# Sixteen expert blocks moved into the last batch's routing, and experts taken in the order of their rows

## The reference, cut to what matters

```
x = x + attention(layernorm(x))            # 16 heads of 16, causal, rotary
t = layernorm(x)
scores = softmax(t @ Wg.T)                 # 16 experts in 4 groups
topi   = top_k(scores, where the two best groups are, 4)
y = sum over the token's 4 experts of scores[e] * (silu(t@W1[e]) * (t@W3[e])) @ W2[e]
z = (silu(t@Ws1) * (t@Ws3)) @ Ws2          # shared expert, every token
x = x + y + z
```

## Time and profile before

| what | value |
|---|---|
| median of three runs | 923.8 us (922.39 to 925.73) |
| profiled execution | 926.76 us, of which the span of the profile is 924.9 us |
| TensorE's granted clock, mean of the span | 0.926 of 2.4 GHz |
| busy: PE / DVE / ACT / POOL | 774.2 / 738.9 / 483.2 / 517.4 us |
| chain of work that ended last | PE 54%, DVE 22%, issue 9%, DMA 7% of the span |

### The profile page before, as it was taken

How to read it: one execution, slowest core, us unless ns; L and a number is a source line. 1 busy time by engine, 2 the same in 40 slices (tenths; PEclk the granted TensorE clock), 3 DMA queues, 4 the chain that set the end, 5 groups by cost and what they waited for, 6 DMA issues and landing times.

```text
span 924.9 us, 20989 instructions
## 1 busy us (share of the span) xinstructions
PE 774.2 (84%) x6103; PEld 692.3 (75%) x6103; DVE 738.9 (80%) x2558; ACT 483.2 (52%) x1236; POOL 517.4 (56%) x512
## 2 busy tenths in 40 slices
PE   3668999999999999999988663899999999999600
PEld 3556788878788878887876552799999999999600
DVE  4556789889998899889967774898888888888534
ACT  4244565645454555555545432666666666666400
POOL 4123334656555655655545473577777777777600
PEclk9779999999999999999999865999999999999855
DMA  3656674567655765567521664978888888888598
GB/s 120 156 145 162 185 195 125 184 193 227 153 185 182 222 170 181 174 193 203 138 77 62 223 242 143 263 149 137 139 139 135 141 137 140 136 136 141 72 377 348
DMA packets 111998, 157.90 MB, mean 171 GB/s; under 512 B 13072, under 2 KB 94992, under 8 KB 111888
## 3 DMA queue, kind: packets, MB, share of 16 engines
q1 hardware_dynamic: 84000, 115.52, 43.0%
q0 software_dynamic: 26736, 36.85, 23.3%
q10 hardware_dynamic: 1152, 4.19, 1.1%
HBM read 74.55 MB, written 81.43 MB: 169 GB/s over the span
## 4 chain that ended last, share of the span: by engine, by line
PE 54%; DVE 22%; issue 9%; DMA 7%; SPq 3%; ACT 2%; POOL 2%; another core or an unknown queue 0%; DVEq 0%; POOLq 0%; ACTq 0%
PE bank L570 25%; PE bank L827 8%; DVE row_max L1121 4%; PE bank L610 4%; PE bank L794 3%; PE bank L614 3%; PE bank L654 3%; DMA acc<-acc_scr 2%; PE bank L638 2%; SPq L551 2%; DMA acc_scr<-yb,token 2%; DVE ropeds_lo L1067 2%; DVE rope_b L1107 2%; PE bank L577 2%; DVE wexp L1067 2%
## 5 line engine op out<-in xcount | busy, mean ns | idle before, releaser
L1534 POOL DMA_INDIRECT acc_scr<-yb,token x143 | 226.3, 1582 | 83.0 <-DMA acc_scr<-yb,token 36.9
L1503 POOL DMA_INDIRECT rows_scr<-xn,rows_of x128 | 128.4, 1003 | 61.9 <-issue 31.1
L570 PE MATMUL bank<-wexp,xbT_hi 128*128 x572 | 151.6, 347 | 4.9 <-DVE xbT_lo L1067 4.3
L1121 DVE TENSOR_REDUCE row_max<-bank 128x2 f32<-128x512 f32 (+1 forms) x192 | 128.9, 682 | 25.9 <-PE bank L614 24.9
L907 ACT ACTIVATE probs<-bank 128x512 f32<-128x512 f32 x192 | 110.7, 607 | 38.9 <-PE bank L654 30.8
L827 PE MATMUL bank<-wexp,upT 112*128 (+1 forms) x572 | 121.5, 305 | 0.3 <-DVE upT L1067 0.2
L610 PE MATMUL bank<-kst,qst 112*128 112x256 f32 (+1 forms) x512 | 98.8, 299 | 23.9 <-DMA kst<-qk_scr 18.8
L610 PEld LDWEIGHTS bank<-kst,qst 112*128 112x128 f32 x512 | 79.4, 199 | 38.8 <-DMA kst<-qk_scr 20.1
L1483 POOL TENSOR_SCALAR_AFFINE_SELECT probs<-probs 128x1024 f32<-128x1024 f32 x64 | 70.2, 1097 | 67.1 <-ACT probs L907 65.9
L570 PEld LDWEIGHTS bank<-wexp,xbT_hi 128*128 128x128 f32 x572 | 94.5, 192 | 7.8 <-issue 7.7
L654 PE MATMUL bank<-qst,kst 114*128 114x512 f32 (+1 forms) x256 | 84.1, 391 | 14.6 <-issue 9.3
(11 more groups left out here) (201 smaller groups left out, 2252.5 us busy)
## 6 DMA issues: line engine op xcount, KB each, us to landing
xb<-rows_scr SPq DMA_DIRECT2D x143, 138.0 KB
qk_scr<-ropeds_hi SPq DMA_DIRECT2D x64, 256.0 KB, 2.5
qst<-qk_scr SPq DMA_DIRECT2D x64, 192.0 KB
kst<-qk_scr SPq DMA_DIRECT2D x64, 192.0 KB
acc<-acc_scr SPq DMA_DIRECT2D x24, 512.0 KB, 14.5
st<-in_wexp SPq DMA_DIRECT2D x16, 608.0 KB
qk_scr<-ropeds_lo SPq DMA_DIRECT2D x32, 256.0 KB, 2.9
acc_scr<-zero SPq DMA_DIRECT2D x10, 768.0 KB
```

Of the source, the lines that this page charges most:

```text
L570: ins = e.matmul(region, stationary(s, k), moving(m, k), start=(j == 0), stop=(j == n - 1), skip_group_check=True)
L1121: e.tensor_reduce(row_max[:, half, h:h + n, i], view, AX.X, ALU.max).then_inc(s_max)
L1503: e.indirect_dma_start(rows_scr[:, :], bass.IndirectOffsetOnAxis(ap=rows_of[b % 2][:, i, r:r + 1].bitcast(U32), axis=0), x2[:, i, :], None ...
L1534: e.indirect_dma_start(acc_scr[j % NACC][:, :], bass.IndirectOffsetOnAxis(ap=token[j % NW][:].bitcast(U32), axis=0), yb[j % NYB][:], None, ...
```

## The change

Some rows are complete before the last batch is routed. After 13 batches (0 to `ORDER_AT` = 12) 13312 pairs are placed. The fullest expert then has at least 832 rows, six whole blocks, whatever the data; the second at least 666 (five), the third 476 (three), the fourth 256 (two). So `SURE` is [6, 5, 3, 2], and `AHEAD` = 16 blocks can go without the last three batches' rows. The other 127 (`LISTED`) are listed by the tables as before.

- **Order of the experts.** A new stage `order` of 6 steps, in the list behind `mix` step 5 of the last batch, ranks the experts by their rows after 13 batches (12 small DVE instructions, four small matmuls in two groups). An expert's weights are now loaded into the slot of its rank: SP reads the expert's number from `slot_w` before each load.
- **Blocks ahead.** A new stage `ahead` of 80 steps, five for a block, stands in the list from the last batch's `route` step 11 on. In it each engine's part of block j stands at a fixed distance: SP's row loads from step 0, PE at 5j, 5j+6, 5j+12 and 5j+18, ACT and DVE behind them, POOL's addition at 5j+29. `route` steps 12 to 38 of the last batch, the end of its `shared` and the `tables` steps stand between these steps. The blocks' PSUM banks come from the plan.
- **Weights.** Four experts (8 halves) instead of seven are prepared before the blocks; the four loads are issued at once. The other twelve (24 halves) stand one behind every third block, from block 16 to block 85, and the waits in `hidden` follow from the order (`slots_for`).
- **`chosen`.** Its two additions in each batch move from POOL to DVE, in `route` steps 21 and 22.
- **Zeros.** The 16 `zero_tail` DMAs are issued in `tables` steps 3 to 6, and the first row load of block 16 waits for all of them.
- **Shifts in the list.** `shared` of the last two batches starts later by 0.25 and 0.32 of a batch's length; `route` of the last three moves by up to 0.03. `tables` has one DVE instruction and two matmuls more.

The diff, cut to its core:

```diff
-SOONER = {"route": [-0.15, -0.3, -0.45]}
+SOONER = {"route": [-0.14, -0.28, -0.42], "shared": [0, 0.25, 0.32]}
...
-    runs += [[B - 1 + 5.2, 0.700 / 8, "tables", B - 1, 8], ...
-             [B - 1 + 2.799, 3.12 / 60, "experts", 0, 1000]]
+    runs += [[B - 1 + 5.28, 0.880 / 8, "tables", B - 1, 8], ...
+             [B - 1 + 2.35, 1.67 / EXPERT_STEPS, "experts", 0, EXPERT_STEPS],
+             [ORDER_AT + 6.09, 0.25 / 6, "order", 0, 6],
+             [B - 1 + 5.0, 1.63 / (5 * AHEAD), "ahead", 0, 5 * AHEAD]]
...
-ON_ATTEND = 7
-EXPERT_STEPS = 5 * ON_ATTEND
-BETWEEN = [(h * (E - 1) // (2 * (E - ON_ATTEND)), ON_ATTEND + h // 2, h % 2) for h in range(2 * (E - ON_ATTEND))]
+ORDER_AT = 12
+SURE = [-(-((ORDER_AT + 1) * S * (TOPK - x)) // (E - x)) // P for x in range(TOPK)]
+SLOT_OF = [x for x in range(TOPK) for _ in range(SURE[x])]
+AHEAD = len(SLOT_OF)
+LISTED = NBLK - AHEAD
+EXPERT_STEPS = 5 * TOPK
+PARTS = {'x': (0, 1, 2, None), 'h': (6, 8, 9, None), 't': (12, 13, 14, None), 'y': (18, 19, None, 29)}
+BETWEEN = [(AHEAD + 3 * h, TOPK + h // 2, h % 2) for h in range(2 * (E - TOPK))]
...
             def load_expert(x):
                 w.wait_ge(s_wexp, 2 * (x - NST + 1))
-                e.dma_start(st[x % NST][:], a["wexp"][x]).then_inc(d_w[x % NST], 16)
+                w.wait_ge(s_order, ORDERED)
+                at = e.value_load(slot_w[0:1, x:x + 1], min_val=0, max_val=(E - 1) * P)
+                e.dma_start(st[x % NST][:], a["wexp"][bass.ds(at, P), :]).then_inc(d_w[x % NST], 16)
...
+            def load_rows(j):
+                if j < AHEAD:
+                    x = SLOT_OF[j]
+                    w.wait_ge(s_order, ORDERED)
+                    at = e.value_load(slot_row[0:1, x:x + 1], min_val=0, max_val=(E - 1) * CAP)
+                    at = at + (j - SLOT_OF.index(x)) * P
+                    for i in range(NXN):
+                        w.wait_ge(d_rows[i], 128 * len(range(i, ORDER_AT + 1, NXN)))
+                else:
+                    ...
+                    w.wait_ge(d_tail, 16 * E)
+                    for i in range(NXN):
+                        w.wait_ge(d_rows[i], 128 * (B // NXN))
...
             def hidden(j):
-                w.wait_ge(s_wexp, 2 * min(j + 1, E))
+                w.wait_ge(s_wexp, 2 * slots_for(j))
...
                 elif k == 21:          # route, DVE
                     ...
+                    if b > ORDER_AT:
+                        w.wait_ge(s_order_pe, 1)
+                    w.wait_ge(s_const, 9)
+                    e.tensor_tensor(chosen[:], chosen[:], picks[:, 0, :], ALU.add).then_inc(s_chosen0)
                 elif k == 22:
                     ...
+                    w.wait_ge(s_chosen0, b + 1)
+                    e.tensor_tensor(chosen[:], chosen[:], picks[:, 1, :], ALU.add).then_inc(s_chosen)
...
-                elif k == 21:          # route, POOL
-                    w.wait_ge(s_ranked, b + 1)
-                    e.tensor_tensor(chosen[:], chosen[:], picks[:, 0, :], ALU.add).then_inc(s_chosen0)
-                    w.wait_ge(s_chosen0, b + 1)
-                    e.tensor_tensor(chosen[:], chosen[:], picks[:, 1, :], ALU.add).then_inc(s_chosen)
...
+                elif stage == "ahead":     # POOL
+                    if k == 0:
+                        w.wait_ge(d_zero, 16 * len(ZEROS))
+                        for i in range(2):
+                            w.wait_ge(d_base[i], 16 * len(range(i, ORDER_AT + 1, 2)))
+                    for _, j in parts_at(3, k):
+                        add(j)
```

More of the change, by code:

```diff
@@ L54 @@
 NXB, NYB, NST, NW = 6, 6, 4, 10
-NTAIL = 4
 NF, TF = 8, 4
@@ L97 @@
     "route": {20: ["rank"]},
+    "order": {0: ["od"]},
+    "tables": {0: ["cb"], 5: ["eb"]},
+    "ahead": {},
 }
@@ L106 @@
     "route": {21: ["rank"]},
+    "order": {5: ["od"]},
+    "tables": {5: ["cb"]},
+    "ahead": {},
 }
@@ L125, in plan @@
             continue
-        if stage == "experts":
-            if ("attend", B - 1) not in done:
-                continue
+        if stage in ("experts", "ahead", "tables") and ("attend", B - 1) not in done:
+            continue
+        if stage in ("experts", "ahead") and k == 0 and ("order", 0) not in done:
+            continue
+        if stage == "order" and k == 0 and ("ranks", ORDER_AT) not in done:
+            continue
         if stage == "tables" and k == 0 and ("ranks", B - 1) not in done:
@@ L511, in sync_program @@
                     find_tails()
-                    zero_tail(0)
-                    zero_tail(1)
+                elif stage == "tables" and k in (3, 4, 5, 6):
+                    for x in range(4 * (k - 3), 4 * (k - 2)):
+                        zero_tail(x)
+                elif stage == "ahead":
+                    ahead(k)
                 elif stage == "load":
@@ L761, in tensor_program, with blocks @@
+            def blocks(n):
+                for kind, j in parts_at(0, n):
+                    if kind == "x":
+                        turn_rows(j)
+                    elif kind == "h":
+                        hidden(j)
+                    elif kind == "t":
+                        turn_hidden(j)
+                    else:
+                        result(j)
             for stage, b, k in order:
@@ L831, in tensor_program @@
-            fetch_weights(0)
-            for s in range(NBLK + 3):
-                if s < NBLK:
-                    turn_rows(s)
-                if 0 <= s - 1 < NBLK:
-                    hidden(s - 1)
-                if 0 <= s - 2 < NBLK:
-                    turn_hidden(s - 2)
-                if 0 <= s - 3 < NBLK:
-                    result(s - 3)
+                elif stage == "ahead":
+                    blocks(k)
+            fetch_weights(AHEAD)
+            for n in range(5 * AHEAD, LAST_STEP):
+                blocks(n)
@@ L1042, in scalar_program @@
[L1042 to L1053 removed]
+                    behind_attention(w)
@@ L1055, in scalar_program @@
+                    expert_hi(k // 5, k % 5 // 2)
+                elif stage == "ahead":
+                    behind_attention(w)
+                    blocks(k)
+            for n in range(5 * AHEAD, LAST_STEP):
+                blocks(n)
             out_rows = out.rearrange("b s d -> (b s) d")
@@ new lines, in blocks @@
+            def blocks(n):
+                for kind, j in parts_at(2, n):
+                    if kind == "x":
+                        gathered(j)
+                    elif kind == "h":
+                        hidden(j)
+                    else:
+                        hidden_lo(j)
+                for at, x, half in BETWEEN:
+                    if 5 * at + 4 == n:
+                        if x == BEHIND:
+                            behind_all(w)
+                        expert_lo(x, half)
```

539 lines of the change are left out of this document (326 added, 213 removed).

## The result

The changed kernel took 913.34 us (median of 4 runs, 911.80 to 914.24) where the kernel before took 924.53 us (median of 4). The ratio is 0.988, 95% interval 0.9856 to 0.9904. That is faster, by 11.2 us where 22.0 were forecast, and outside the range of 892 to 912 us. The profiled execution took 914.24 us, its span is 912.5 us.

The account below looks back on a forecast made before the run. PE bounds the blocks at 2.00 us each; DVE is busiest in the hole before. Block 16 sooner 23.0, less 1.0 for halves, less 0 for the first phase: 22.0 us off the 923.8 us median, 901.8 us; range 892 to 912.

Parts of the forecast that it names:

- Block 16's place: When block 16 reaches DVE: 590.7 us instead of 613.73 us, 23.0 us sooner; the number that sets the change's worth.
- Block 0: Part 1, DVE's queue up to the first block's token copy: 549.0 us against 570.88 us before.
- The sixteen blocks: Part 2, block 0 to block 16: DVE bound, 36.7 us of work plus 5 us idle, bounds 0 and 12.
- SP's queue: Row loads, zero fills and four weight loads ahead of block 16's row load: taken to cost 0.
- The clock: PE's granted clock: 0.50 when PE starts on the blocks ahead, about 1.00 soon after some 550 us.
- The wait for the first weights: DVE's 2.06 us wait before block 0 moves behind `order` but stays the same: 0, bounds 2 less and 3 more.
- The last batch's rows in time: The last batch's scattered rows in SBUF for block 16 by 584.5 to 590.5 us, just under 590.7; thin cover.
- The first rival: The last batch's rows come late behind POOL's additions: block 16 at 599 us, 910 us in all; chance 0.18.
- Part 3: Behind block 16, 24 weight halves, one behind every third block: hidden under PE, 1 us in all, bounds 0 and 10.8.
- Part 4, the first phase: `chosen`'s additions moved from POOL to DVE in 13 batches: 0, bounds 2 us gained and 5 us lost.
- The rival that this edit pays in every batch: First phase: `chosen`'s additions on DVE collide with POOL's work, 1.9 us a batch, 25 us, 927 us; chance 0.04.
- The end: The 59 us after the last block's token copy (last additions, three sums, output) stay as they are.

Follow-up runs that it names:

- e5: The kernel before with only the two additions into `chosen` of each batch moved from POOL to DVE; ratio 1.0032 to the kernel before.
- f1: The changed kernel with both engines' halves in quarters, 8 result buffers instead of 6 and 12 token buffers instead of 10; 890.06 us, ratio 0.9785 to the kernel before.
- h1: The changed kernel with both engines' halves in quarters and the sixteen sure blocks a batch's length later in the order; 901.55 us, ratio 0.9909 to the kernel before.
- h3: The changed kernel with both engines' halves in quarters and the sixteen sure blocks' steps 14% closer together; ratio 0.9783 to the kernel before.
- e7: The changed kernel with ACT's half moved behind `xbT_hi` and 8 result buffers instead of 6; ratio 0.9829 to the kernel before.
- r_after: The changed kernel itself, unedited, run again beside its edited versions; 900.12 us, ratio 0.9857 to the kernel before.
- r_q2: The changed kernel with both engines' halves in quarters, run again beside the unedited changed kernel; 893.81 us, ratio 0.9793 to the kernel before.
- e1: The changed kernel with ACT's half moved from directly ahead of `xbT_hi` to directly behind it; 906.7 us, ratio 0.9795 to the kernel before.
- m0: The changed kernel with both engines' halves for slots 4 to 15 writing 8 columns only, listed blocks using slot 0's weights; ratio 0.9792 to the kernel before.
- q2: The changed kernel with both engines' halves cut into quarters, ACT's directly behind `xbT_hi`; ratio 0.9794 to the kernel before.

## Why the prediction was right or wrong

- **Block 16's place** (590.7 us): right, 590.33, with some luck. The first phase came out shorter: the last copy of the attention's output (ACT, `oT`) started at 507.78 us, 1.99 us sooner than before (509.77). Nothing in the forecast had that, and it can be the spread between executions: e5, f1, h1 and h3 in one set had it between 496.18 and 498.39 us. Behind that point the change gained 21.4 us, not 23.4. Inside the rest two errors cancelled. Block 0 was at 544.88, not 549.0. The sixteen blocks took 45.45 us, not 41.7: DVE worked 32.40 us, not 36.7, and was idle for 13.05 us, not 5, just over my upper bound of 12. Part of the missing work is that of the blocks still in flight at block 16, which I had counted in full (DVE had done `upT` for 14 of the 16); the rest isn't taken apart. The idle time lies in pieces of up to 2.05 us, most of them ended by nothing that the trace names, while PE waits for `xbT_lo` four times, up to 1.0 us: the fixed order among five engines, named as the point of most risk. Neither a denser order (h3) nor more buffers (e7) changed it much. In a second execution (r_after) the sixteen blocks took 42.20 us, with 31.57 us of DVE's work, and one wait stands out: 2.74 us for the rows of block 12, which SP loads between zero fills and weight loads. r_q2 had it with 2.98 us and f1 with 1.91 us. I had put SP's queue at nothing; how much of the time these waits cost no run shows. The clock was 1.00 as forecast from 544.88 to 560 us, then 0.89, 0.84 and 0.92 in the three stretches of 10 us up to 590 us, PE busy for 6.87 and 7.95 us in the first two.
- **The wait for the first weights** (0, bounds -2 and 3): block 0 came 4.1 us sooner than forecast, 2.0 of them from the first phase, so no loss shows here. Where I had put 3.9 us for `order`, its twelve DVE instructions ran between 512.56 and 515.42 us with eight of `route` and `mix` among them: no wait of their own.
- **The last batch's rows in time**: right. The last scatter began at 572.35 us and block 16's row load was no one's wait. The first rival, 910 us, fell near the result by luck: its mechanism, late rows, is not what cost the time.
- **Part 3, the failed step.** DVE's 5.99 us for three blocks and a half against PE's 6.00 were read as just hidden, 1 us in all. It cost 12.4 us in the profiled execution. The bound of 24 x 0.45 = 10.8 us was near the truth, and a little low. Two errors stand in the term. First, a sum over three blocks says that DVE can catch up; it doesn't say that PE doesn't wait meanwhile. PE is the bound and has no slack: what it waits once is lost. What counts is whether one burst on DVE (0.71 us) fits in the time by which `xbT_lo` is ahead of PE. The trace has 0.63 us of lead of which 0.49 us can be used; what is over that is 0.22 us, and e1 lost 0.26 to 0.30 us a half. With quarters (0.39 us) hardly anything was lost; no run has a size between. The earlier trace rows were misread: the first interval of 2.07 us is `xbT_lo` using up its lead (L570 started 0.56 us behind its end at 603.46 us and 0.14 us behind it at 605.53 us), and 2.45 to 2.48 us is the price for good. Second, I costed DVE's half and forgot ACT's, which every move of a half carries with it; it stands ahead of `xbT_hi`, and DVE's slack went into 0.54 us of waiting. So the lead was not rebuilt between two halves: `xbT_lo` at 604.40 us, two blocks behind a half, ended 0.15 us ahead of L683 (604.97 us). ACT is busy for only 68% of the time (163.87 of 242.16 us), which says nothing of who waits behind its 0.70 us.
- **Part 4, the first phase** (0, bounds -2 and 5): in e5 3.9 us, within the bounds. The rival that this edit pays in every batch was right in sign for the kernel before, 3.9 / 16 = 0.24 us a batch where 1.9 were priced. Whether that is the collision of that rival no row shows. In the changed kernel it isn't settled.
- **The end**: as forecast; the last copy of tokens to the end of the span is 912.5 - 854.0 = 58.5 us.

The sum by the trace is then closed: 613.73 to 865.80 us before, 252.07 us all PE, against 590.33 to 854.04 us, 263.71 us. Gained 23.4, lost 11.6, remain 11.8 of 924.9 - 912.5 = 12.4 us; the rest lies in the end. The same question put to the medians of one set gives 6.3 us for the halves, so between 6 and 12 us of the loss are shown to be theirs, by which of the two measures one takes.

## What to carry to other kernels

Work slipped between the steps of a pipeline whose bound has no slack must be costed by its longest single burst against the lead of the step behind it, on every engine that has a share in it, and not by its mean. The lead has to be rebuilt before the next burst comes. If it doesn't fit, cut it smaller and spread it: here the same weights in quarters cost 0.07 to 0.13 us of the bound's time where halves cost 0.52 us. Place it behind the instruction for which another engine waits, not ahead of it: here that alone took 0.54 us of DVE's waiting away in each round.

## What the runs showed of the hardware that was not expected

- With DMA at 0.89 to 0.90 of its time busy, an addition to the sums at times landed so late that ACT waited up to 2.5 us for it with six buffers in turn (m0, 10.6 us in all); in another execution of nearly the same work (q2) it waited 0.4 us in all.
- The same kernel's median differed between sets by up to 16 us (910.3 to 926.2 us), more than the change was worth. Two of the sets, 912.7 and 923.6 us, were on the same chip, so it is not the chip alone, as the expectation of r_after has it. The difference lies in the first phase: in e5's execution the last `oT` copy started at 497.83 us, 11.9 us sooner than in the kernel before, and the 72 blocks behind block 16 took 143.96 us in both.
- Quarters of 304 columns took 0.48 us against 0.79 us for halves of 608, and 0.39 against 0.71 us from start to start: cutting in two cost 0.07 us.
